# An audio tower on one core: stores issued by SyncE, wider gaps at ScalarE's waits, the tokens' first result thirty beats earlier

## The chip, the cores and the metric

The program runs on one core of one Trainium2 chip. The metric is device time in microseconds (us) of one execution. The engines are TensorE (PE, with weight loads as PEld), VectorE (DVE), ScalarE (ACT), GpSimd (POOL) and SyncE (SP). They run one instruction stream each and meet at semaphores.

## The reference

128 sequences of 256 steps and 64 channels go through a token stage, two attentions and two feed-forward layers:

```python
h = _L0_tok_ref(x, ...)                          # strided conv, norm over time and channels, PReLU -> (128, 128, 64)
h = h + _L0_attn_ref(_layernorm(h), W)           # x_ = xn triu(W)^T; (x_ xn^T) xn
h = h + _L0_ffn_ref(_layernorm(h), ...)          # product keys, below
h = h + _L1_attn_ref(_layernorm(h), ...)         # linear attention, 8 heads of 8, then a norm
h = h + _L1_ffn_ref(_layernorm(h), ...)          # 8 experts, top 2, gelu

# _L0_ffn_ref
sim = einsum('pbnhd,pkhd->pbnhk', q, pk_keys)    # 2 sides, 8 heads, 64 sub-keys
scores, idx = top_k(sim, 16)
score = scores[0][..., :, None] + scores[1][..., None, :]
final_scores, pk_idx = top_k(score, 16); final_scores = softmax(final_scores)
k = einsum('bnhk,bnhkd->bnhd', final_scores, keys_table[ind])    # 4096 rows per head
v = einsum('bnhk,bnhkd->bnhd', final_scores, values_table[ind])
out = softmax(causal(q_ k^T)) v; return out @ Wo
```

## The kernel before

**Pairs and periods.** Two sequences make a pair; there are 64 (`PAIRS`). Every engine works through periods, one per pair. In a period it interleaves the work of several pairs (`over_pairs`): `dense` and `prep` of the pair itself, `tail` and `back` of the pair before (its last beats, attention, second attention, experts, output), `select` of the next pair (sub-key products, top 16) and `front` of the one behind that (convolution to first attention).

**Beats.** The bulk of the product-key layer is done densely for six of eight heads. A period has 192 beats (`BEATS`), 32 for each such head. In beat c TensorE forms 128 x 512 sums in one of three PSUM banks (L1425, L1426, `p_s`), ScalarE takes their exponential into `ew` (L1174), VectorE masks four beats at once (L947), and nine beats later (`LAG`) TensorE multiplies the result with the value table (L1437, `p_d`). So a late exponential holds the sums three beats later, and a late mask holds the product. The mask of the beats 188 to 191, for instance, is needed for the product in beat 5 of the next period. After each head ScalarE empties `p_d` into `dense_t_sb` (L1179), and TensorE can start the next head's products only then.

**The order.** Each step of a chain yields its due beat, and `interleave` emits on each engine always the step that is due first. Nothing else sets the order: an engine runs its stream in this order, and an instruction that waits stops all behind it. The due beats of `front` are spread by shares in `FRONT`, those of `back` in `BACK` (from beat 16 to 190), those of `select` by `at_select` and `at_unit`, those of the rank matrices by `at_fill`. Steps that the text speaks of:

- `exponent` (ScalarE, due at c + 1), `mask` (VectorE, due at c + 1.5).
- `neg_kmax` (VectorE L999) and `ek_t` (ScalarE L1268, waits for it), due at `BACK["kmax"]` 101.2 and `BACK["ek"]` 104.3.
- The tokens' first result `h0` (VectorE L726 to L737, with L684 to L696): due at `FRONT["h0"]` 146.1 and 148.1. The scale that it needs comes from ScalarE's `root1` (141.2), that of its normalisation `xh1` (159.5) from `root2` (155.9).
- The rank matrices for a head: `rank_hot` (VectorE L928 twice, L935 twice), then 32 matmuls (L1388).
- The experts: 16 matmuls (L1573) and eight gelus (L1296) due at `BACK["hid"]` 171.0, 32 matmuls (L1580) at `BACK["y"]` 180.0, and on VectorE the output stage L1081, L1086 (183.0, 184.5), L1089 and L1092 (186.0), which writes `h_out` and signals `out_ready`.
- The store: ScalarE waits for `out_ready` (L1301) and issues the DMA (L1302), due at 190.0, between two exponentials.
- The queries (TensorE L1479), due at beat 1 of the period, wait for `out_ready` too, since they overwrite the bank `p_x` that the output stage reads.
- Gathered heads: GpSimd fetches rows (L642) and adds them up (L656, L659), from beats 164.5, 172, 179.5 and 187.
- SyncE loads the inputs (L535) and the value table in 48 pieces of 256 KB per period (L543) through a ring of four; piece u waits until the products of piece u - 4 are done.

## Time and profile before

| | |
|---|---|
| Median of 3 runs | 13503.45 us (13494.18 to 13523.84) |
| Profiled execution, its own time | 13459.08 us |
| Its span | 13457.3 us |
| Mean granted TensorE clock | 0.959 |
| PE / DVE / ACT / POOL busy | 89 / 82 / 75 / 49 % |
| A period in the middle | about 208 us |

The profile is of one execution. Its span is the time from the first to the last instruction; 1.8 us lie around it. A period is 192 beats, so a beat takes 1.08 us on average. L numbers are lines of the kernel before. In the timeline a number in brackets is idle time of the engine before the instruction, with what ended it. Where the text says "beat 105" it means the stretch between the sums of beat 105 and those of 106, found by counting L1426 in the timeline; in the period that is shown here beat 105 starts at 6444.9 us, beat 153 at 6495.4, beat 191 at 6541.7.

### The profile page before, as it was taken

Reading aid. Unit: us, or ns where it says so; the run is one execution under the profiler, and the core shown is the slowest. Engines: PE = TensorE matmul, PEld = TensorE weight load, DVE = VectorE, ACT = ScalarE, POOL = GpSimd, SP = SyncE. Lnnn points to the kernel's source line nnn. Section 1 sums busy time; section 2 is a strip of 40 time slices with the busy share of each in tenths; the row PEclk is TensorE's granted clock in tenths of the full one; section 3 lists DMA queues with packets and bytes.
Section 4 is the critical chain, followed back from the end, with each engine's and each line's share of the span. In section 5 each row is a group of like instructions: output and inputs, shape, how many; then the busy total and the mean of one; then the engine's idle time right before and its main releaser. Section 6 shows DMA issues by size and latency. Waiting matters only on the chain.

```text
span 13457.3 us, 332297 instructions
## 1 busy us (share of the span) xinstructions
PE 12006.3 (89%) x83744; PEld 9072.3 (67%) x83744; DVE 11075.8 (82%) x37953; ACT 10064.7 (75%) x24019; POOL 6548.1 (49%) x5160
## 2 busy tenths in 40 slices
PE   6998988989989889898998988988989899899898
PEld 4666666666666666666666666666666666666666
DVE  7888888888888888888888888888888888888885
ACT  5777777777777777777777777777777777777776
POOL 4454444544444445444454444544544445545453
PEclk9999999999999999999999999999999999999998
DMA  2222222222222222222222222222222222222222
GB/s 72 85 84 81 87 81 83 85 81 86 82 81 85 81 84 83 81 86 81 84 85 80 87 82 82 85 82 85 82 82 86 81 84 84 82 86 83 83 87 64
DMA packets 612231, 1111.70 MB, mean 83 GB/s; under 512 B 134096, under 2 KB 150992, under 8 KB 610384
## 3 DMA queue, kind: packets, MB, share of 16 engines
q1 hardware_dynamic: 461648, 816.40, 19.8%
q0 software_dynamic: 131072, 268.70, 7.1%
q8 instruction: 887, 14.53, 0.4%
q14 instruction: 928, 7.60, 0.2%
q10 hardware_dynamic: 17696, 4.46, 0.1%
HBM read 1084.90 MB, written 4.19 MB: 81 GB/s over the span
## 4 chain that ended last, share of the span: by engine, by line
PE 58%; DVE 17%; ACT 11%; DVEq 7%; issue 6%; ACTq 0%; POOL 0%; POOLq 0%
PE p_d L1437 25%; PE p_s L1425 6%; PE p_s L1426 6%; ACT ew L1174 5%; PE p_g L1388 4%; DVE ew L947 4%; PE p_f L1372 2%; PE p_x L1580 2%; PE p_x L1516 2%; PE p_x L1573 1%; DVEq L685 1%; ACT gath L1217 1%; ACT prob L1247 1%; DVE h_out L1092 1%; DVE cand L827 1%
## 5 line engine op out<-in xcount | busy, mean ns | idle before, releaser
L1174 ACT ACTIVATE ew<-p_s 128x512 f32<-128x512 f32 x12288 | 7012.6, 617 | 2393.0 <-PE p_s L1426 1882.8
L1437 PE MATMUL p_d<-ew,tab 128*128 128x256 f32 x24576 | 7739.6, 398 | 639.2 <-DVE ew L947 347.5
L642 POOL DMA_INDIRECT gath<-in_table,idx x4096 | 4947.5, 1208 | 5234.6 <-PE p_s L1426 4827.6
L947 DVE SCALAR_TENSOR_TENSOR ew<-ew 128x1024 f32<-128x1024 f32 x3072 | 4024.2, 1310 | 1483.8 <-ACT ew L1174 1389.8
L1437 PEld LDWEIGHTS p_d<-ew,tab 128*128 128x128 f32 x24576 | 3827.4, 196 | 1094.3 <-issue 908.7
L1425 PE MATMUL p_s<-mov,rank_sel 128*128 128x256 f16 x12288 | 3418.5, 278 | 439.2 <-ACT ew L1174 438.2
L1426 PE MATMUL p_s<-mov,piece_sel 128*128 128x256 f16 x12288 | 3415.4, 278 | 0.0
L656 POOL TENSOR_TENSOR gath<-gath 128x1024 f32<-128x1024 f32 (+2 forms) x768 | 1338.7, 1743 | 1538.4 <-PE p_s L1426 1443.8
L1426 PEld LDWEIGHTS p_s<-mov,piece_sel 128*128 128x128 f16 x12288 | 1221.1, 99 | 1242.8 <-issue 85.4
L1425 PEld LDWEIGHTS p_s<-mov,rank_sel 128*128 128x128 f16 x12288 | 1241.6, 101 | 1098.2 <-issue 763.9
L1217 ACT ACTIVATE gath<-gath,kv_w 128x128 f32<-128x128 f32 x4096 | 1452.2, 418 | 0.0
L928 DVE TENSOR_TENSOR rank_hot<-iota_k,rank_key 128x2048 f16<-128x2048 f16 x768 | 977.6, 1280 | 41.7 <-issue 23.4
L1388 PE MATMUL p_g<-ident_rank,rank_hot 128*128 128x128 f16 x12288 | 866.2, 227 | 117.2 <-DVE rank_hot L935 71.1
L1388 PEld LDWEIGHTS p_g<-ident_rank,rank_hot 128*128 128x128 f16 x12288 | 790.1, 102 | 178.8 <-issue 160.1
L1165 ACT CAST mov<-p_g 128x512 f16<-128x512 f32 (+1 forms) x1152 | 606.9, 527 | 170.1 <-PE p_g L1388 168.6
L935 DVE TENSOR_TENSOR rank_hot<-rank_hot,rank_val 128x1024 f16<-128x1024 f16 x768 | 523.3, 688 | 19.9 <-issue 6.4
L776 DVE FIND_INDEX8 top_i<-top,sim 128x8 uint32<-128x64 f32 x2048 | 411.5, 219 | 0.0
L768 DVE MAX8 top<-sim 128x8 f32<-128x64 f32 x2048 | 296.3, 212 | 138.2 <-ACT sim L1153 137.8
L1247 ACT ACTIVATE prob<-p_x,neg_max 128x128 f32<-128x128 f32 x1024 | 399.7, 436 | 12.1 <-DVE neg_max L972 12.1
L798 DVE FIND_INDEX8 top_i<-top,sim 128x8 uint32<-128x64 f32 x2048 | 406.9, 219 | 0.0
L784 DVE MATCH_REPLACE8 sim<-top,sim 128x64 f32<-128x64 f32 x2048 | 403.4, 207 | 0.0
L793 DVE MAX8 top<-sim 128x8 f32<-128x64 f32 x2048 | 300.9, 212 | 4.6
(234 smaller groups left out, 12275.6 us busy)
## 6 DMA issues: line engine op xcount, KB each, us to landing
tab<-in_dense_t SPq DMA_DIRECT2D x3072, 256.0 KB
gath<-in_table,idx POOLq DMA_INDIRECT x4096
xin<-in_x SPq DMA_DIRECT2D x64, 128.0 KB, 2.4
out<-h_out ACTq DMA_DIRECT2D x64, 64.0 KB, 1.7
row_consts<-in_rows SPq DMA_DIRECT2D x1, 548.0 KB, 4.2
w_sb<-in_w SPq DMA_DIRECT2D x1, 512.0 KB, 6.9
w_sb<-in_w ACTq DMA_DIRECT2D x1, 256.0 KB, 4.5
gath<-in_wqpk_t SPq DMA_DIRECT2D x1, 256.0 KB, 5.5
```

The lines of the kernel that those rows point to most:

```text
L642: G.indirect_dma_start(out=gath[:, slot, k, :], out_offset=None, in_=table[:, :], in_offset=bass.IndirectOffsetOnAxis(ap=idx[pair.par][:, ...
L656: G.tensor_tensor(gath[:, slot, 0:half, :], gath[:, slot, 0:half, :], gath[:, slot, half:2 * half, :], ALU.add).then_inc(halved, 1)
L928: V.tensor_tensor(hots[p].rearrange("t r s c i -> t (r s) c i"), iota_k[:, :].rearrange("t (c i) -> t c i", i=2)[:, None, :, :].to_broadca ...
L947: V.scalar_tensor_tensor(four[:, :, 2 * T:4 * T], four[:, :, 0:2 * T], CHOSEN, four[:, :, 2 * T:4 * T], ALU.is_gt, ALU.mult).then_inc(dens ...
L1165: A.copy(mov[mov_slot(d)][:, first:last, :].rearrange("q a t -> q (a t)"), p_g[:, 0:2 * T * (last - first)]).then_inc(bank_free, 1)
L1174: A.activation(ew[:, c % EW_RING, :], p_s[c % PS_RING][:, :], ACT.Exp).then_inc(dense_e_ready, 1)
L1217: last = A.activation(gath[:, slot, k, :], gath[:, slot, k, :], ACT.Copy, scale=kv_w[pair.par][:, HEADS * p + h, k:k + 1])
L1247: last = A.activation(prob[:, a, hp, :], px[:, a, T * hp:T * hp + T], ACT.Exp, bias=neg_max[:, h:h + 1], accum_out=row_sum[:, a, hp:hp + 1])
L1388: last = M(p_g[:, T * p:T * p + T], rank_hot[p][:, r, :, :].rearrange("t s i -> t (s i)"), ident_rank[:, r, :], start=(r == 0), stop=(r == ...
L1425: M(bank[:, 0:2 * T], rank_sel[:, c % CHUNKS, :], mov[mov_slot(d)][:, 0, :], start=True, stop=True)
L1426: M(bank[:, 2 * T:4 * T], piece_sel[:, k, :], mov[mov_slot(d)][:, MAP_OF[layout], :], start=True, stop=True).then_inc(pair_mm, 1)
L1437: last = M(p_d[:, 0:2 * T], tab[:, u % TAB_RING, i, :], ew[:, c % EW_RING, 2 * T:4 * T], start=(k == 0), stop=(k == CHUNKS - 1))
```

## The change

Stores: SyncE gets a `store` that waits for `out_ready` and issues the DMA, placed behind the 48 table pieces of the period and ahead of the next input and the next table pieces; ScalarE's wait, store and final wait go. The queries wait for a new semaphore `y_taken`, signalled by L1081, the first step of the output stage (and once ahead of the loop); the wait for `out_ready` goes to the transposes of the keys (`k_tr`, beat 16).

Due beats:

| step | before | after |
|---|---|---|
| FRONT var, root1, h0, root2 | 121.7, 141.2, 146.1, 155.9 | 105.9, 113.2, 118.0, 127.8 |
| FRONT xh1 and all behind it | 159.5 ... | the same |
| BACK ek, a, l1_x, z, h3, xn, gap, mix, hid | 104.3 ... 171.0 | each 2.0 later |
| BACK y, out | 180.0, 183.0 | 183.5, 187.0 |
| queries' copy on ScalarE | 2.0 | 2.4 |
| sub-key units 1 to 3: matmul, copy | u - 1.9, u - 0.8 | u - 4.0, u - 2.4 |
| sub-key units on VectorE | u | u + 0.4 |
| rank_hot, all four steps | | each 1.0 earlier |

```diff
-               "xin_tr:3 x2t:3 conv:8 stats:6 mean:6 dev:20 var:16 root1:4 h0:8 root2:3 xh1:4 gram:2 gram_copy:2 "
+               "xin_tr:3 x2t:3 conv:8 stats:6 mean:6 dev:7 var:6 root1:4 h0:8 root2:26 xh1:4 gram:2 gram_copy:2 "
...
-EARLY = {"queries": 1, "q_copy": 2}
-BACK = spread(TAIL_END + 1, BEATS - 2,
+EARLY = {"queries": 1, "q_copy": 2.4}
+BACK = spread(TAIL_END + 1, BEATS - 5,
...
-              "gap:5 gap_e:3 mix:6 hid:9 y:3 out:7 store")
+              "gap:5 gap_e:3 mix:6 hid:10.5 y:3.5 out")
...
+        def store(pair):
+            hold(sp, out_ready, pair.n + 1)
+            sp.dma_start(of_pair(out_pairs, pair.n), h_out[pair.par][:, :, :]).then_inc(out_done[pair.par], 16)
...
                 tables(Pair(2 * it + q + 1, it + q, 1 - q))
+                store(Pair(2 * it + q, it, q))
...
-                yield at_unit(u, 0)
+                yield at_unit(u, 0.2)
...
-                yield at_fill(d, 0) + 2 * p - 9.2
+                yield at_fill(d, 0) + 2 * p - 10.2
...
-                yield at_fill(d, 0) + p - 5.2
+                yield at_fill(d, 0) + p - 6.2
...
-                            ALU.add)
+                            ALU.add).then_inc(y_taken, 1)
...
-                yield at_unit(u, 0) - 0.8
+                yield at_unit(u, 0) - (0.8 if u == 0 else 2.4)
...
-            yield BACK["store"]
-            hold(act, out_ready, count)
-            act.dma_start(of_pair(out_pairs, pair.n), h_out[pair.par][:, :, :]).then_inc(out_done[pair.par], 16)
...
-                yield at_unit(u, 0) - 1.9
+                yield at_unit(u, 0) - (1.9 if u == 0 else 4)
...
-            if positive(done):
-                hold(pe, out_ready, done)
+            hold(pe, y_taken, done + 1)
...
             hold(pe, q_ready, count)
+            if positive(done):
+                hold(pe, out_ready, done)
```

Three places show how the streams move. In the changed kernel the same statements stand some lines further down (L1174 is L1185, L947 is L957, L1092 is L1102).

ScalarE around beat 190, before; the register and ISA rows are the waits' bookkeeping:

```order
L1173 REGISTER_ALU
L1174 ACTIVATE ew<-p_s 128x512
L1302 ISA
L1302 DMA out<-h_out 128x2x64
L1173 REGISTER_ALU
L1174 ACTIVATE ew<-p_s 128x512
```

and SyncE at the end of a period, after:

```order
L544 DMA tab<-in_dense_t 128x512
L549 ISA
L549 DMA out<-h_out 128x2x64
L536 ISA
L536 DMA xin<-in_x 128x2x128
L514 ISA
L544 DMA tab<-in_dense_t 128x512
```

The store has left ScalarE's exponentials and stands on SyncE behind the last table piece of one period and ahead of the first of the next.

VectorE at the end of the output stage (`k_t` is the experts' output buffer, L945 and L955 belong to the masks), before, where L1081 and L1086 stand six instructions further up with a mask and a normalisation of `front` between:

```order
L1089 TENSOR_REDUCE xh<-k_t 128x128
L1091 ISA
L1092 TENSOR_TENSOR h_out<-h,xh 128x128 [waits out_done0]
L945 REGISTER_ALU
L947 SCALAR_TENSOR_TENSOR ew<-ew 128x4x256 [waits dense_e_ready]
L926 REGISTER_ALU
L928 TENSOR_TENSOR rank_hot<-iota_k,rank_key 128x2048 [waits map_tr]
```

after:

```order
L1091 TENSOR_TENSOR k_t<-p_x,row_consts 128x1024 [waits y_mm]
L1096 TENSOR_TENSOR k_t<-k_t,w_full 128x1024
L955 REGISTER_ALU
L957 SCALAR_TENSOR_TENSOR ew<-ew 128x4x256 [waits dense_e_ready]
L1099 TENSOR_REDUCE xh<-k_t 128x128
L1101 ISA
L1102 TENSOR_TENSOR h_out<-h,xh 128x128 [waits out_done0]
L936 REGISTER_ALU
L938 TENSOR_TENSOR rank_hot<-iota_k,rank_key 128x2048 [waits map_tr]
L955 REGISTER_ALU
L957 SCALAR_TENSOR_TENSOR ew<-ew 128x4x256 [waits dense_e_ready]
```

The mask that stood behind the output's last step (that of the beats 184 to 187) now stands ahead of its third; one mask (180 to 183) and the normalisation of `front` have moved ahead of its first.

VectorE at beats 117 to 120 (`prob_t` is `l1_x`, `f_tmp`, `yn` and the last `h` are the tokens' first result), before:

```order
L855 TENSOR_TENSOR kv_w<-fin_d,fin_r 128x256
L1011 TENSOR_TENSOR prob_t<-p_x,head_of 128x1024 [waits l1_o_mm]
L862 CAST pos_h<-pos_i 128x64
L866 TENSOR_TENSOR sim<-iota_c,pos_h 128x1664
L945 REGISTER_ALU
```

after:

```order
L865 TENSOR_TENSOR kv_w<-fin_d,fin_r 128x256
L736 ISA
L694 SCALAR_TENSOR_TENSOR f_tmp<-p_f,f_rstd 128x2 [waits f_root_ready]
L696 SCALAR_TENSOR_TENSOR f_tmp<-f_tmp,f_rstd 128x2
L698 SCALAR_TENSOR_TENSOR f_rstd<-f_tmp,f_rstd 128x2
L739 SCALAR_TENSOR_TENSOR yn<-yn,f_rstd,row_consts 128x64 x2
L1021 TENSOR_TENSOR prob_t<-p_x,head_of 128x1024 [waits l1_o_mm]
L743 SCALAR_TENSOR_TENSOR neg_part<-yn,row_consts 128x128
L745 SCALAR_TENSOR_TENSOR h<-yn,neg_part 128x128
L703 BN_STATS f_stats<-h 128x6 x2
L706 BN_AGGR f_mv<-f_stats 128x2 x2
L872 CAST pos_h<-pos_i 128x64
```

The eleven instructions of `h0` stand here now, thirty beats ahead of where they stood.

## Rows read from the trace of the kernel before

**Rows 1.** Totals: the page's first part (busy us, share of the span, instructions).
```profile
PE 12006.3 (89%) x83744; PEld 9072.3 (67%) x83744; DVE 11075.8 (82%) x37953; ACT 10064.7 (75%) x24019; POOL 6548.1 (49%) x5160
```
**Rows 2.** Waits, whole run: who waited for whom; us, times, longest us.
```profile
PE p_s L1425 <- ACT ew L1174: 438.2, 315, 5.2
PE p_d L1437 <- DVE ew L947: 347.5, 258, 4.2
ACT ew L1174 <- DVE h_out L1092: 345.2, 61, 5.9
ACT ek_t L1268 <- DVE neg_kmax L999: 269.6, 63, 4.4
DVE top L768 <- ACT sim L1153: 137.8, 126, 3.8
```
**Rows 3.** Windows of one period, its beats 84 to 154.
```profile
core 0: us, PE busy (x) PEld busy (x) DVE busy (x) ACT busy (x) POOL busy (x), PEclk, DMA share, GB/s
6429.00:6453.00 24.00, 18.90 (x128) 14.56 (x127) 22.25 (x106) 15.51 (x37) 12.37 (x10) 0.94 0.31 92
6453.00:6470.00 17.00, 17.00 (x136) 13.43 (x134) 11.54 (x29) 14.51 (x38) 7.46 (x7) 0.99 0.31 91
6470.00:6500.00 30.00, 24.20 (x166) 17.69 (x165) 27.08 (x82) 21.80 (x53) 9.10 (x7) 0.96 0.28 87
```
**Rows 4.** Timeline, beats 103 to 106: start, duration, instruction, count, [idle before, releaser].
```profile
6443.50 0.27 PE L1425 MATMUL p_s<-mov,rank_sel 128*128 128x256 f16 x1
6444.15 0.27 PE L1425 MATMUL p_s<-mov,rank_sel 128*128 128x256 f16 x1
...
6450.22 1.19 PE L1437 MATMUL p_d<-ew,tab 128*128 128x256 f32 x2 [2.84 <-ACT dense_t_sb L1179]
...
6448.87 0.37 ACT L1268 ACTIVATE ek_t<-p_x,neg_kmax 128x128 f32<-128x128 f32 x1 [4.35 <-DVE neg_kmax L999]
```
**Rows 5.** Timeline, TensorE at beat 153.
```profile
6498.46 1.19 PE L1437 MATMUL p_d<-ew,tab 128*128 128x256 f32 x2 [2.84 <-DVE ew L947]
```
**Rows 6.** Timeline, TensorE at the end of the period (beats 191, 0, 1).
```profile
6547.05 0.37 PE L1425 MATMUL p_s<-mov,rank_sel 128*128 128x256 f16 x1 [4.65 <-ACT ew L1174]
...
6548.41 2.08 PE L1479 MATMUL p_x<-xh_t,wq_sb 64*128 64x128 f32 x16
```
**Rows 7.** Windows behind the three long waits: granted clock (PEclk) and busy time.
```profile
6450.30:6453.80 3.50, 3.50 (x22) 2.97 (x23) 2.43 (x17) 1.27 (x4) 0.94 (x1) 0.56 0.00 0
6498.50:6505.00 6.50, 6.50 (x22) 4.46 (x23) 5.58 (x28) 2.87 (x8) 0.00 (x0) 0.53 0.00 0
6545.50:6551.00 5.50, 3.95 (x23) 2.95 (x24) 5.34 (x5) 2.53 (x5) 4.92 (x4) 0.50 0.20 60
```
**Rows 8.** Timeline, VectorE and GpSimd in the output stage, beats 180 to 0.
```profile
6534.35 1.22 DVE L1081 TENSOR_TENSOR k_t<-p_x,row_consts 128x1024 f32<-128x1024 f32 x1 [2.64 <-PE p_x L1580]
6535.65 1.79 DVE L1086 TENSOR_TENSOR k_t<-k_t,w_full 128x1024 f32<-128x1024 f32 x1
...
6540.43 1.90 DVE L1089 TENSOR_REDUCE xh<-k_t 128x128 f32<-128x1024 f32 x1
...
6542.41 3.14 DVE L1092 TENSOR_TENSOR h_out<-h,xh 128x128 f32<-128x128 f32 x1
...
6543.03 2.36 POOL L656 TENSOR_TENSOR gath<-gath 128x1024 f32<-128x1024 f32 x1
...
6547.84 1.74 DVE L928 TENSOR_TENSOR rank_hot<-iota_k,rank_key 128x2048 f16<-128x2048 f16 x1
6549.50 1.47 DVE L947 SCALAR_TENSOR_TENSOR ew<-ew 128x1024 f32<-128x1024 f32 x1
```
**Rows 9.** Groups by shape: an addition shaped like L1092, elsewhere; mean ns.
```profile
L1027 DVE TENSOR_TENSOR h<-h,xh 128x128 f32<-128x128 f32 x64 | 18.7, 293 | 4.8
```
**Rows 10.** DMA issues: KB each, median us from issue to landing.
```profile
xin<-in_x SPq DMA_DIRECT2D x64, 128.0 KB, 2.4
wq_sb<-in_wq SPq DMA_DIRECT2D x1, 256.0 KB, 5.0
```

More of the change, by code:

```diff
@@ L502, in build @@
     y_mm = sem("y_mm")
+    y_taken = sem("y_taken")
     out_ready = sem("out_ready")
@@ L556, in _ @@
             tables(Pair(n, n // 2, n % 2))
+            store(Pair(n - 1, (n - 1) // 2, (n - 1) % 2))
+        store(Pair(PAIRS - 1, (PAIRS - 1) // 2, 1))
+        for p in range(2):
+            sp.wait_ge(out_done[p], 16 * (PAIRS // 2) + 16)
     @block.gpsimd
@@ L1096, in _ @@
         dve.wait_ge(pool_consts, POOL_CONSTS)
+        dve.sem_inc(y_taken, 1)
         V.reciprocal(rank_inv[:, :], rank_left[:, :])
@@ L1146, in select @@
             count = pair.n + 1
-            yield EARLY["q_copy"] + 1
+            yield EARLY["q_copy"] + 0.8
             act.wait_ge(xh2_tr, count)
@@ L1299, in back @@
             A.preload_act_table_set("natural_log_exp_and_others")
-            yield BACK["store"]
-            hold(act, out_ready, count)
-            act.dma_start(of_pair(out_pairs, pair.n), h_out[pair.par][:, :, :]).then_inc(out_done[pair.par], 16)
         over_pairs(act, front, select, prep, tail, back, weigh, sums, dense)
-        for p in range(2):
-            act.wait_ge(out_done[p], 16 * (PAIRS // 2) + 16)
     @block.tensor
```

2 rows, old and new, of the table BACK are left out of this document.

## The prediction

> **What bounds the kernel.** I began with the totals: TensorE is busy 12006 us of 13457, VectorE 11076 [rows 1]. No engine is full, so the time above TensorE's own work is waiting, and a static order makes it repeat in each of the 64 periods. Next the waits of the whole run, to see what holds TensorE [rows 2]: 438 us for exponentials (L1425), 348 us for masks (L1437). The same list shows ScalarE idle for 345 us at its store's wait (61 times, 5.7 us each) and for 270 us at `ek_t` (63 times, 4.3 us each). Then the timeline of one period, to see where TensorE loses how much. A beat in the steady stream takes 0.65 us, from one L1425 to the next [rows 4], though the period's mean is 1.08. Three places stand out: 2.84 us in beat 105, with ScalarE idle 4.35 us for `neg_kmax` ahead of the exponentials and of the emptying of `p_d` [rows 4]; 2.84 us in beat 153 for a late mask [rows 5]; 4.65 us at the end of the period, for exponentials that stand behind the store [rows 6]. Behind each of the three the granted clock is 0.50 to 0.56, the lower of its two levels (1.2 instead of 2.4 GHz) [rows 7], while in a stretch without a long wait it is 0.99 [rows 3]. At the lower level the work takes twice as long, so half of TensorE's busy time there is lost: 3.50 x 0.44 = 1.5 us, 6.50 x 0.47 = 3.1 us and 3.95 x 0.50 = 2.0 us [rows 7]. Waits and clock together make 2.8 + 1.5, 2.8 + 3.1 and 4.65 + 2.0, some 17 us of a period of 208.
>
> The Trainium skill ("TensorE: Matmul & The Clock Gate", What's actually happening) has the clock gated down by default and released by activity; the trace agrees: the three low stretches begin in TensorE's three longest waits.
>
> **The store, and the end of the period.** ScalarE's wait and issue go; its exponentials of beats 189 to 191 follow their sums at once. Gain on TensorE: the 4.65 us [rows 6] and the 2.0 us of clock. What is late next is VectorE. `out` is due four beats later, and the mask of beats 188 to 191 stands behind all of it. From the end of the experts' last matmuls VectorE has 1.22 + 1.79, a mask of 1.47, 1.90, 3.14, `rank_hot` 1.74 and that mask 1.47 [rows 8]: 12.7 us. TensorE reaches the product that needs it after 13.5 beats of 0.65 (8.8), the queries (2.08 at half clock [rows 6], so 1.0), and about two beats' worth (1.3, an estimate) for a transposition and the first sub-key matmuls: 11.1 us. So a new wait of 1.6 us in beat 5. The term is 4.65 + 2.0 - 1.6 = 5.0 us, times 61 = **305 us**. Bounds: 2.0 (the clock stays low and the new wait is 2.7) and 6.6 (no new wait).
>
> **The store on SyncE.** It costs nothing as long as the table is early. The last step of the output ends 1.22 + 1.79 + 1.47 + 1.90 + 3.14 = 9.5 us after those matmuls [rows 8]. Queued behind the store are the input of a later pair and the next period's first table pieces, for which only TensorE waits. Landing takes between 2.4 us (128 KB) and 5.0 us (256 KB, at the start, with many others) [rows 10]; with about 1 us for issuing store, input and piece, the first piece lands 13 to 15.5 us after the matmuls. Its product is due four beats and a rank matrix after the product above, at 12.7 + 2.6 + 1 = 16 us. Cover: 0.8 to 3.4 us. The wait of `k_tr` for `out_ready` in beat 16 lies later still: nothing.
>
> **Beats 84 to 154: `ek` two beats later, `h0` thirty earlier, `rank_hot` one earlier.** ScalarE now does two exponentials and empties `p_d` before it waits for `neg_kmax`, which VectorE reaches no sooner. The products of beat 105 then wait only for their mask: about 0.8 us is left of the 2.84, and the 1.5 us of clock comes back: 3.5 us by beat 109. At beat 153 the wait (2.84) and the clock (3.1) could go too, 9.5 us in all, if VectorE let them. It doesn't. In rows 3 it is busy 22.3 of 24, 11.5 of 17 and 27.1 of 30 us: full before 6453 and after 6470, idle for 5.5 us only between, while TensorE is busy all of those 17 us. The moved block, eleven small instructions and their drains, some 2.8 us by its share of the third stretch (an estimate), goes from the full stretch to the idle one. So the mask in beat 153 comes at least 2.8 us earlier (the block alone) and at most 5.5 us (all idle time filled, which TensorE's 3.5 us of head start makes possible). I take 4.4, four fifths of the idle time, since a mask still waits for its exponential now and then. Behind beat 154 VectorE stays full up to beat 160, so the clock's 3.1 us there is not a second gain. New short waits of about 1.5 us appear near beats 125 and 133, where the block delays masks; they are in the 4.4. Times 63 = **277 us**. Bounds: 2.0 (only the wait in beat 105) and 7.
>
> **The rest.** The sub-key units' matmul and copy come earlier: VectorE's 138 us of waiting for `sim` [rows 2] goes, 2.2 us per period, but TensorE does not wait there, so 0.3 us (0 to 2). The experts two beats later move eight gelus and two table loads behind a copy that frees a bank: -0.2 us (-1.5 to 0.5). Together 63 x 0.1 = **6 us**.
>
> **Sum.** 305 + 277 + 6 = 588 us. Against the profiled execution that is 13459 - 588 = 12871; the median of the runs lies 44 us above that execution, which gives 13503 - 588 = **12915 us**.
>
> **Rivals.**
> - *VectorE is not the limit* (0.14). If its instructions pack tighter than I count, TensorE gains 6.6 x 61 + 7 x 63 = 844 us: 12660. For it: VectorE is idle 18% of the run [rows 1]. Against: the full stretches in rows 3.
> - *The clock stays low* (0.13). The shorter waits that remain could still pull it down: the first term loses 2.0, the second about 1: 588 - 122 - 63 = 403, so 13100. For it: a remaining wait of 1.6 us stands in beat 5. Against: rows 3 have 0.99 over 17 us with small waits around.
> - *The port shared with GpSimd* (0.10). L1092 takes 3.14 us [rows 8], an addition of its shape elsewhere 0.29 [rows 9]; it ends when GpSimd's first sum (L656) does. Later by four beats, the output stage can meet the second sum as well. Then its last step takes up to 2.4 us more and TensorE waits that long in beat 5: 588 - 2.4 x 61 = 442, so 13061. The Trainium skill ("SBUF — State Buffer", Who interferes with whom) calls the shared ports an exclusive lock, held for a whole instruction; by that rule the step waits out any sum that began before it.
> - *Only the store pays* (0.07). The masks eat what `ek` and `h0` give: 305 - 100 = 200 us, 13300.
> - *The queue of SyncE makes it slower* (0.03). Table pieces stand behind a wait for VectorE. If the last output step comes more than 3.4 us later than I count, TensorE waits for the first piece, us for us; it decides from there, and more than 3.4 + 9.6 = 13 us late it takes all the gain. At 15 us late: 61 x 2 = 120 us slower, 13625. Against it: no row of VectorE in the output stage waits that long [rows 8].
> - *Nothing happens* (0.03). The order of another engine holds the exponentials as before: 13500.
>
> **The numbers.** My forecast has 0.50. The chance of faster by over 0.2% (27 us, about what a measurement of this kernel can tell from no change) is 0.50 + 0.14 + 0.13 + 0.10 + 0.07 = 0.94; within it 0.03; slower 0.03. The range goes from 12700, close to the first rival and to both upper bounds, to 13200, past the clock and the port; it leaves out the last three cases and little of the first.
>
> **What the profile will show.** No ScalarE wait for L1092; TensorE's wait for exponentials down from 438 us to under 150; `ek_t`'s wait at or above 4 us still, but without TensorE behind it; TensorE's wait for masks not much smaller than 348, and moved to beats 5, 125 and 133; VectorE's share up to about 86%; granted clock above 0.98; periods of 198 to 200 us. I am wrong if a piece of `tab` ends TensorE's waits, if the clock still falls three times a period, or if the period stays above 205 us.

## The result and the profile after

| | before | after |
|---|---|---|
| Median | 13512.54 us of 4 runs (13494.18 to 13523.84) | 13668.67 us of 4 runs (13642.79 to 13680.1) |
| Ratio | | 1.0114, 95% interval 1.0095 to 1.0134 |
| Profiled span | 13457.3 us | 13640.9 us |
| Mean granted clock | 0.959 | 0.953 |
| A period | 208.2 us | 211.0 us |

The change makes the kernel 1.1% slower. The forecast was 12915 us, 4.4% faster, with a range up to 13200: wrong in sign. L1185 is L1174 of before, L957 is L947, L1102 is L1092, L1009 is L999, L1443 is L1437, L712 is L702, L925 is L915, L666 is L656, L1356 is L1350, L1431 and L1432 are L1425 and L1426.

First the waits of the whole run after the change, the view of [rows 2] (us in total, times, longest):

```profile
ACT ew L1185 <- PE p_s L1432: 2492.4, 2328, 5.5
...
PE p_d L1443 <- DVE ew L957: 581.9, 332, 5.3
PE p_s L1431 <- ACT ew L1185: 200.4, 304, 3.1
ACT ek_t L1279 <- DVE neg_kmax L1009: 181.0, 63, 2.9
PE p_f L1356 <- DVE xh L712: 161.9, 61, 24.6
PE p_g L1394 <- ACT kv L1196: 156.1, 62, 2.6
```

ScalarE's wait for the output stage is gone, and TensorE's wait for exponentials has fallen from 438 to 200 us. In their place TensorE waits 582 us for masks (348 before), and two small lines have grown: the gram matmul L1356 waits for the normalisation `xh1` 61 times (4 times before), and the matmuls of the rank matrices wait 156 us for `kv` (40 before). So time was moved, and more than was gained. Where, a table by beats tells; it is made from the starts of each beat's second sum (L1426 before, L1432 after) in the timeline, averaged over periods 4 to 59:

| beats | before | after | difference |
|---|---|---|---|
| 0 to 15 | 16.6 | 20.0 | +3.4 |
| 15 to 84 | 73.0 | 72.9 | -0.1 |
| 84 to 109 | 26.8 | 24.7 | -2.1 |
| 109 to 124 | 13.6 | 12.1 | -1.5 |
| 124 to 152 | 25.5 | 29.4 | +3.9 |
| 152 to 163 | 13.8 | 8.3 | -5.5 |
| 163 to 170 | 6.2 | 13.6 | +7.5 |
| 170 to 184 | 22.5 | 23.9 | +1.4 |
| 184 to 192 | 10.2 | 6.1 | -4.2 |
| period | 208.2 | 211.0 | +2.8 |

The places of the forecast did gain: beats 152 to 163 give 5.5 us, beats 184 to 192 give 4.2 (and the first four beats of the next period 1.8 more), beats 84 to 109 give 2.1 of the 3.5 forecast there. The largest loss, beats 163 to 170, is in no term of it. There the timeline of one period after shows VectorE and GpSimd:

```profile
6613.75 2.67 DVE L712 TENSOR_SCALAR xh<-h,f_mv,f_rstd 128x64 f32<-128x64 f32 x2
6616.35 0.55 DVE L921 TENSOR_TENSOR rank_val<-rank_n,rank_inv 128x384 f16<-128x384 f16 x1
6616.81 2.38 DVE L925 CAST rank_key<-top_i 128x192 f16<-128x192 uint32 x4
6619.35 1.28 DVE L957 SCALAR_TENSOR_TENSOR ew<-ew 128x1024 f32<-128x1024 f32 x1
...
6614.03 2.34 POOL L666 TENSOR_TENSOR gath<-gath 128x1024 f32<-128x1024 f32 x1 [17.00 <-PE p_s L1432]
6616.55 1.46 POOL L666 TENSOR_TENSOR gath<-gath 128x512 f32<-128x512 f32 x1 [0.18 <-POOL gath L666]
6618.19 0.72 POOL L666 TENSOR_TENSOR gath<-gath 128x256 f32<-128x256 f32 x1 [0.18 <-POOL gath L666]
```

and TensorE in the same stretch:

```profile
6616.57 0.30 PE L1356 MATMUL p_f<-ident,xh 128*128 128x128 f32 x1 [2.24 <-DVE xh L712]
...
6620.93 1.19 PE L1443 MATMUL p_d<-ew,tab 128*128 128x256 f32 x2 [3.18 <-DVE ew L957]
```

GpSimd's first sum starts when TensorE reaches beat 164 (it waits for L1432). VectorE has just begun the two small L712. They take 2.67 us together and end 0.05 us behind the sum's first instruction (6614.03 + 2.34); the four casts L925 take 2.38 us. TensorE waits 2.24 us for `xh`, then 3.18 us for the mask behind the casts. The groups by shape give the mean of one (columns: busy us, mean ns, then idle time), before:

```profile
L915 DVE CAST rank_key<-top_i 128x192 f16<-128x192 uint32 x256 | 54.0, 275 | 0.0
L702 DVE TENSOR_SCALAR xh<-h,f_mv,f_rstd 128x64 f32<-128x64 f32 x128 | 38.5, 344 | 5.1
```

and after:

```profile
L712 DVE TENSOR_SCALAR xh<-h,f_mv,f_rstd 128x64 f32<-128x64 f32 x128 | 158.5, 1281 | 5.0
L925 DVE CAST rank_key<-top_i 128x192 f16<-128x192 uint32 x256 | 148.5, 639 | 0.0
L1102 DVE TENSOR_TENSOR h_out<-h,xh 128x128 f32<-128x128 f32 x64 | 88.0, 1375 | 7.7 <-issue 5.2
```

The two cost 214 us more over the run, with the same shapes and counts, while L1102 has come down to 1375 ns from the 3.14 us of [rows 8]. Windows after, at the two worst places and in one stretch without a long wait (columns as in [rows 3]):

```profile
6453.00:6460.00 7.00, 6.96 (x34) 5.11 (x35) 6.85 (x22) 2.76 (x5) 5.63 (x6) 0.57 0.37 113
6620.90:6627.50 6.60, 6.58 (x24) 4.65 (x25) 6.15 (x13) 3.24 (x8) 0.00 (x0) 0.59 0.05 8
...
6595.00:6613.00 18.00, 17.67 (x114) 12.87 (x113) 16.54 (x64) 16.68 (x38) 1.19 (x1) 1.00 0.28 80
```

The clock is at its lower level behind beats 5 and 165, as it was behind beats 191 and 153 before [rows 7], and full in the 18 us from beat 139 on. By these rows beats 164 and 165 cost 2.24 + 3.18 us of waiting and 6.58 x 0.41 = 2.7 us of clock.

### The profile page after: what moved, and what is told of

It is laid out like the page before. It is cut to its first block, busy times and chain, and to the rows that moved or that the text cites. A ratio compares the mean times of both kernels' runs of the same rounds, so it can differ in the third digit from the quotient of the medians.

```text
span 13640.9 us, 332361 instructions
## 1 busy us (share of the span) xinstructions
PE 12101.2 (89%) x83744; PEld 9104.8 (67%) x83744; DVE 11000.6 (81%) x37953; ACT 10110.7 (74%) x24019; POOL 6393.2 (47%) x5160
## 4 chain that ended last, share of the span: by engine, by line
PE 47%; DVE 23%; DVEq 11%; ACT 10%; issue 8%; ACTq 0%; POOL 0%; another core or an unknown queue 0%; POOLq 0%
PE p_d L1443 21%; DVE ew L957 6%; PE p_s L1432 5%; PE p_s L1431 5%; ACT ew L1185 5%; PE p_g L1394 5%; DVEq L942 3%; DVE rank_hot L938 2%; PE p_x L1523 2%; DVEq L695 2%; PE p_f L1378 1%; DVEq L885 1%; ACT gath L1228 1%; PE p_x L1580 1%; PE p_x L1509 1%
## 5 line engine op out<-in xcount | busy, mean ns | idle before, releaser
L1185 ACT ACTIVATE ew<-p_s 128x512 f32<-128x512 f32 x12288 | 7060.9, 610 | 2722.8 <-PE p_s L1432 2492.4
L1443 PE MATMUL p_d<-ew,tab 128*128 128x256 f32 x24576 | 7825.6, 401 | 612.0 <-DVE ew L957 581.9
L957 DVE SCALAR_TENSOR_TENSOR ew<-ew 128x1024 f32<-128x1024 f32 x3072 | 3867.3, 1261 | 1996.3 <-ACT ew L1185 1722.4
L1443 PEld LDWEIGHTS p_d<-ew,tab 128*128 128x128 f32 x24576 | 3857.0, 198 | 1121.6 <-issue 945.4
L1431 PE MATMUL p_s<-mov,rank_sel 128*128 128x256 f16 x12288 | 3438.1, 280 | 209.4 <-ACT ew L1185 200.4
L1432 PE MATMUL p_s<-mov,piece_sel 128*128 128x256 f16 x12288 | 3433.4, 279 | 0.4 <-issue 0.4
L1432 PEld LDWEIGHTS p_s<-mov,piece_sel 128*128 128x128 f16 x12288 | 1231.2, 100 | 1303.9 <-issue 158.8
L1431 PEld LDWEIGHTS p_s<-mov,rank_sel 128*128 128x128 f16 x12288 | 1255.7, 102 | 840.8 <-issue 499.9
L666 POOL TENSOR_TENSOR gath<-gath 128x1024 f32<-128x1024 f32 (+2 forms) x768 | 1228.5, 1600 | 1188.4 <-PE p_s L1432 1093.3
L1394 PE MATMUL p_g<-ident_rank,rank_hot 128*128 128x128 f16 x12288 | 897.1, 231 | 229.4 <-ACT kv L1196 156.1
L1394 PEld LDWEIGHTS p_g<-ident_rank,rank_hot 128*128 128x128 f16 x12288 | 821.2, 105 | 294.2 <-issue 271.3
L945 DVE TENSOR_TENSOR rank_hot<-rank_hot,rank_val 128x1024 f16<-128x1024 f16 x768 | 510.2, 692 | 19.9 <-issue 6.4
L1258 ACT ACTIVATE prob<-p_x,neg_max 128x128 f32<-128x128 f32 x1024 | 384.5, 405 | 12.1 <-DVE neg_max L982 12.1
L1196 ACT ACTIVATE kv<-p_g,fin_r 128x128 f32<-128x128 f32 x768 | 241.6, 374 | 86.6 <-PE p_g L1452 86.6
L1378 PE MATMUL p_f<-score_w,xh_t 64*128 64x512 f32 x512 | 283.6, 634 | 24.7 <-ACT xh_t L1160 22.3
```

What stands on the lines that cost most here:

```text
L666: G.tensor_tensor(gath[:, slot, 0:half, :], gath[:, slot, 0:half, :], gath[:, slot, half:2 * half, :], ALU.add).then_inc(halved, 1)
L945: V.tensor_tensor(hots[p][:, :, 0, :, :], hots[p][:, :, 0, :, :], rank_val[:, DENSE * p + d, :, None, :].to_broadcast([T, TOPK, SUBKEYS // ...
L957: V.scalar_tensor_tensor(four[:, :, 2 * T:4 * T], four[:, :, 0:2 * T], CHOSEN, four[:, :, 2 * T:4 * T], ALU.is_gt, ALU.mult).then_inc(dens ...
L1185: A.activation(ew[:, c % EW_RING, :], p_s[c % PS_RING][:, :], ACT.Exp).then_inc(dense_e_ready, 1)
L1394: last = M(p_g[:, T * p:T * p + T], rank_hot[p][:, r, :, :].rearrange("t s i -> t (s i)"), ident_rank[:, r, :], start=(r == 0), stop=(r == ...
L1431: M(bank[:, 0:2 * T], rank_sel[:, c % CHUNKS, :], mov[mov_slot(d)][:, 0, :], start=True, stop=True)
```

## The experiments

**Theory P**: TensorE, without its wait in beat 153, reaches beat 164 before VectorE has done `xh1`; GpSimd's first sum then starts in the middle of it, and shares something with it that only one of them can have. **Theory H**: the output stage four beats later is paid in beats 0 to 15. **Rival**: VectorE is the bound, and each gain is given back at the next mask, whatever GpSimd does.

**1. The parts.** `s1_store`: before, with the store on SyncE alone. (Its expectation speaks of `y_taken`; the kernel that ran still had the queries behind `out_ready`. The whole part came later, in s12.)

```diff
+                store(Pair(2 * it + q, it, q))
...
-            yield BACK["store"]
-            hold(act, out_ready, count)
-            act.dma_start(of_pair(out_pairs, pair.n), h_out[pair.par][:, :, :]).then_inc(out_done[pair.par], 16)
```

> Before, with the stores on SyncE and the queries behind y_taken, and no due beat changed. Theory P (the loss of the change comes from GpSimd's sum at beat 164, which takes the port shared with VectorE while xh1 is being normalised) and theory H (it comes from the experts and the output stage being due later): this part alone is good, the 4.65 us wait at beat 191 and its 2.0 us of low clock go, part comes back in beat 5: 4 to 5 us per period, so about 13230 us. Theory S (the store's move itself costs, through VectorE's late masks or SyncE's queue): 13500 or more, with a new wait in beats 4 to 12 as long as the old one.

Measured: 13480.73 us, ratio 0.9989 (0.998 to 0.9999). Beats 184 to 192 gain 3.3 us; 0 to 15 lose 1.3, 15 to 84 1.1, 84 to 109 0.9. A wait at the period's end was removed, and the same time comes up again in pieces.

`s2_front`: before, with FRONT of after alone.

```diff
-               "... dev:20 var:16 root1:4 h0:8 root2:3 xh1:4 ..."
+               "... dev:7 var:6 root1:4 h0:8 root2:26 xh1:4 ..."
```

> Before, with the FRONT shares of the change and nothing else (h0 thirty beats earlier). Theory P: the wait in beat 153 and its clock (5.8 us per period) go, and a wait of 5 to 8 us appears in beats 164 and 165, with L702 taking 2 to 3 us beside GpSimd's L656: 13450 to 13650 us. Theory V (VectorE's order is better by h0's move, GpSimd has no part in it): 13200 to 13300 us, no new wait at 164. Theory H: the same as V.

Measured: 13837.56 us, ratio 1.0248 (1.023 to 1.0265). Beats 152 to 163 gain 5.7 us, 163 to 170 lose 7.1, 124 to 152 lose 2.0, 170 to 184 lose 1.6. The waits of this kernel (line numbers of before) show the long wait at the gram too:

```profile
PE p_d L1437 <- DVE ew L947: 428.6, 316, 5.3
...
PE p_f L1350 <- DVE xh L702: 137.3, 50, 24.6
```

So the move of `h0` is the part that makes the kernel slower, and it brings the wait at the gram. `s3_no_front`: after, with FRONT of before (the same diff turned round).

> The change with the FRONT shares of before (h0 back at beats 146 and 148). Theory P: TensorE is held in beat 153 again (5.8 us), so GpSimd's sum starts after xh1 is ready and the waits of beats 164 and 165 go (7.9 us): 2 us per period faster than the change, about 13540 us, with L712 back at 0.3 us each. Theory V: undoing a good part makes it slower, 13900 us or more.

Measured: 13384.81 us, ratio 0.991 (0.9887 to 0.9933), 155 us below the expected time. The rest of the change is worth 0.9%. The forecast had 311 us for it in its first and last terms, and 3.5 us per period (220 us) by beat 109 in the second: 3.9%. Beats 163 to 170 take 8.4 us here (6.2 before), so not all of their loss has gone. L712 is short again in all but 6 of its 128 instructions, but the sum now meets `rank_hot` and a mask. In one period:

```profile
6471.47 1.22 DVE L957 SCALAR_TENSOR_TENSOR ew<-ew 128x1024 f32<-128x1024 f32 x1
6472.61 3.38 DVE L938 TENSOR_TENSOR rank_hot<-iota_k,rank_key 128x2048 f16<-128x2048 f16 x1
...
6471.65 3.26 POOL L666 TENSOR_TENSOR gath<-gath 128x1024 f32<-128x1024 f32 x1 [21.63 <-PE p_s L1432]
...
6478.82 0.67 PE L1443 MATMUL p_d<-ew,tab 128*128 128x256 f32 x2 [2.77 <-DVE ew L957]
```

**2. GpSimd's sum.** `s4_sums_later`: after, first sum 3.5 beats later, the others 2.5, 1.5 and 0.5.

```diff
-    return SUMS_AT + 7.5 * m
+    return SUMS_AT + 3.5 + 6.5 * m
```

> The change, with GpSimd's four sums due at beats 168, 174.5, 181 and 187.5 in place of 164.5, 172, 179.5 and 187. Nothing moves on the other four engines. Theory P: xh1 is ready before the first sum starts, so the waits in beats 164 and 165 and the low clock behind them go: 5 to 7 us per period, about 13300 us, L712 at 0.3 us each. Theories V and H: no change within 0.3%, 13669 us, and L712 late for another reason.

Measured: 13267.88 us, ratio 0.9828 (0.9812 to 0.9845): a number in the due beats of GpSimd, an engine with half its time idle, takes 400 us from the changed kernel. VectorE and TensorE at beat 164 in this run:

```profile
6417.78 0.54 DVE L712 TENSOR_SCALAR xh<-h,f_mv,f_rstd 128x64 f32<-128x64 f32 x2
...
6418.70 0.76 DVE L925 CAST rank_key<-top_i 128x192 f16<-128x192 uint32 x4
6419.61 1.22 DVE L957 SCALAR_TENSOR_TENSOR ew<-ew 128x1024 f32<-128x1024 f32 x1
...
6418.47 0.30 PE L1356 MATMUL p_f<-ident,xh 128*128 128x128 f32 x1
...
6421.13 0.67 PE L1443 MATMUL p_d<-ew,tab 128*128 128x256 f32 x2 [1.48 <-DVE ew L957]
```

The same instructions take 0.54 and 0.76 instead of 2.67 and 2.38 us; beats 163 to 170 go from 13.6 to 7.6 us. `s5_xh1_earlier` takes the other side away: the sum stays, `xh1` comes earlier.

```diff
-               "... root2:26 xh1:4 ..."
+               "... root2:20 xh1:10 ..."
```

> The changed kernel with the tokens' normalisation xh1 due six beats earlier (153.5 instead of 159.5), everything else as changed, GpSimd's sums where they were. Theory P (the first sum, due at beat 164.5, and VectorE's L712 and L925 share a port, and TensorE waits for them in beat 164): xh1 is done before the sum begins, so L712 is back at about 0.3 us each, the wait of 2.2 us for xh and most of what follows it goes; rank_key's casts still meet the sum. Beats 163 to 170 take 8 to 9 us instead of 13.6; period about 206, time 13350 (13270 to 13450). Rival (what costs is that gram comes before the sum or that the product there waits for its mask, whatever the port does): beats 163 to 170 stay at 13 us, time 13600 to 13700.

Measured: 13464.48 us, ratio 0.9977 (0.9968 to 0.9987), 110 us above the expected middle; beats 163 to 170 take 9.8 us, where 8 to 9 were expected. L712 is back at 311 ns. But now the sum meets the mask of beats 156 to 159:

```profile
6507.09 3.15 DVE L957 SCALAR_TENSOR_TENSOR ew<-ew 128x1024 f32<-128x1024 f32 x1
6510.16 2.28 DVE L938 TENSOR_TENSOR rank_hot<-iota_k,rank_key 128x2048 f16<-128x2048 f16 x1
...
6506.67 2.48 POOL L666 TENSOR_TENSOR gath<-gath 128x1024 f32<-128x1024 f32 x1 [18.04 <-PE p_s L1432]
6509.33 2.03 POOL L666 TENSOR_TENSOR gath<-gath 128x512 f32<-128x512 f32 x1 [0.18 <-POOL gath L666]
```

A mask of 1.22 us takes 3.15, and TensorE waits 2.58 us for it. The cost is not in `xh1` alone; it is in whatever VectorE does when the sum starts, if TensorE is close behind. `s7_sums_only` is the control: the kernel before, with the sums of s4.

> The kernel before with only GpSimd's sums moved (first sum 3.5 beats later, second 2.5, third 1.5, fourth 0.5), as the control for the run that moved them in the changed kernel. Theory P: before, TensorE came to beat 164 after VectorE had finished xh1, so there is no collision to take away: 13450 to 13530, the same as before within 0.3%. Rival (the sums stand in a bad place whatever the change does): as much gain as in the changed kernel, 2.9%, 13100.

Measured: 13524.26 us, ratio 1.0024 (1.0014 to 1.0034). Where TensorE comes late to beat 164, next to nothing is to be had there (beats 163 to 170 go from 6.2 to 5.9 us), and the run is 0.2% slower. Theory P stands: from both sides, and with its control. What the two engines share these runs do not show by themselves; they show that an instruction of one is held while one of the other runs.

**3. What is left.** `s9_nofront_sums`: s4 with FRONT of before.

> The changed kernel with the sums later and the tokens' result h0 back at beat 146. With the sums out of the way h0's move should be worth what it gains in beats 152 to 158 (5 us) less what it costs in beats 124 to 152 (about 3 us): undoing it loses 2 us per period, 13268 + 63 x 2 = 13390 (13330 to 13450). Rival (h0's move is worth nothing even without the collision, since VectorE has the same work): 13270 or less.

Measured: 13277.95 us, ratio 0.9838 (0.9821 to 0.9854), the same as s4. So the move of `h0` is worth nothing even without the collision: 4.5 us gained in beats 152 to 163 against 3.0 lost in 124 to 152 and 1.5 in 163 to 170. In this the rival was right and I was not.

`s8_out_back`: s4 with the experts, their second layer and the output stage due as before.

```diff
-              "gap:5 gap_e:3 mix:6 hid:10.5 y:3.5 out")
+              "gap:5 gap_e:3 mix:4 hid:9 y:3 out:7 end")
```

> The changed kernel with the sums later, and the experts, their second layer and the output stage due as before (170.9, 180.0, 183.0 instead of 173.0, 183.5, 187.0); ek to mix stay two beats later. Theory H (the output stage four beats later makes the masks of beats 184 to 191 late, TensorE waits in beats 5 and 12 and the clock falls): beats 4 to 15 go from 16.3 back to about 12.3 us, beats 170 to 184 lose 1 us; against that up to 1 us in the last beats. Period 200 to 201, time 13000 (12930 to 13120). Rival (beats 4 to 15 are long because TensorE arrives there sooner, with VectorE behind, wherever the output stage is due): 13268 as without this edit, within 50 us.

Measured: 13273.68 us, ratio 0.984 (0.9823 to 0.9856), no gain. Beats 0 to 15 fell from 20.6 to 17.4 us as theory H says, but 184 to 192 rose by 2.2 and 15 to 84 by 1.7. VectorE and GpSimd, beats 180 to 187 of this run:

```profile
6430.98 2.70 DVE L1096 TENSOR_TENSOR k_t<-k_t,w_full 128x1024 f32<-128x1024 f32 x1
6433.83 2.07 DVE L957 SCALAR_TENSOR_TENSOR ew<-ew 128x1024 f32<-128x1024 f32 x1
...
6430.21 2.38 POOL L666 TENSOR_TENSOR gath<-gath 128x1024 f32<-128x1024 f32 x1
6432.77 2.04 POOL L666 TENSOR_TENSOR gath<-gath 128x512 f32<-128x512 f32 x1 [0.18 <-POOL gath L666]
```

Here the third sum, 1.5 beats later, meets the output stage: L1096 takes 2.67 us on average over this run, 1.23 in s4. `s10_sums_two` puts the second, third and fourth sum back:

```diff
-    return SUMS_AT + 3.5 + 6.5 * m
+    return SUMS_AT + (3.5, 7.5, 15, 22.5)[m]
```

> As the run with the sums later and the output stage back, but only the first sum is later (168); the others stand where they stood (172, 179.5, 187). There the third sum (181) began with the output stage: L1096 took 2.70 us instead of 1.79, the mask behind it 2.07 instead of 1.23, and TensorE lost 2 us in beat 189 and 1.5 us in beats 17 to 20. Theory P: with the third sum ahead of the output stage both come back: beats 189 to 192 at 3 us, beats 15 to 84 at 72.9; period 201.5, time 13050 (12980 to 13150). Rival (the output stage meets a sum wherever it stands, and the masks of beats 180 to 191 stay late): 13274 as before within 50 us, with L1102 longer again in place of L1096.

Measured: 13018.33 us, ratio 0.9675 (0.9661 to 0.9689), within 32 us of the expected middle. Beats 184 to 192 gain 1.2 us and 15 to 84 2.6, and L1096 is down to 1.60 us. The three sums were not moved one by one.

`s11_h0_early` moves `h0` into a hole of VectorE.

```diff
-               "... dev:7 var:6 root1:4 h0:8 root2:26 ..."
+               "... dev:5 var:5 root1:4 h0:8 root2:29 ..."
```

> As s10, with the tokens' result h0 due at 114.4 instead of 118.0, so that it comes into the 1.8 us in which VectorE is idle ahead of the mask of beats 112 to 115, instead of between that mask and the next. Theory V (each block of VectorE costs what it delays the next mask by; h0 at 118 adds 2.9 us ahead of the mask that beat 125 needs, more than TensorE's lead): the wait in beat 125 goes from 1.85 to under 0.5, beats 124 to 152 from 29.4 to 27 us; 60 x 2.4 = 140 us less than s10. Rival (VectorE has as much to do on both sides of that mask, the wait moves to beat 117 or stays): within 30 us of s10.

Measured: 12920.22 us, ratio 0.9603 (0.9588 to 0.9618). VectorE and TensorE around beat 124, in s10:

```profile
6253.90 1.23 DVE L957 SCALAR_TENSOR_TENSOR ew<-ew 128x1024 f32<-128x1024 f32 x1 [1.80 <-ACT ew L1185]
...
6256.32 0.16 DVE L694 SCALAR_TENSOR_TENSOR f_tmp<-p_f,f_rstd 128x2 f32<-128x2 f32 x1
...
6261.76 2.36 DVE L957 SCALAR_TENSOR_TENSOR ew<-ew 128x1024 f32<-128x1024 f32 x2
...
6263.28 0.67 PE L1443 MATMUL p_d<-ew,tab 128*128 128x256 f32 x2 [1.85 <-DVE ew L957]
```

and VectorE in s11:

```profile
6190.54 0.15 DVE L694 SCALAR_TENSOR_TENSOR f_tmp<-p_f,f_rstd 128x2 f32<-128x2 f32 x1
...
6194.29 1.23 DVE L957 SCALAR_TENSOR_TENSOR ew<-ew 128x1024 f32<-128x1024 f32 x1 [0.16 <-issue]
...
6199.16 2.36 DVE L957 SCALAR_TENSOR_TENSOR ew<-ew 128x1024 f32<-128x1024 f32 x2
```

The hole of 1.80 us ahead of the mask is filled, and between the two masks 4.87 us pass instead of 7.86 (from start to start). TensorE does not wait in beat 125 any more; beats 124 to 152 take 27.4 instead of 29.4 us. The same block, 3.6 beats sooner, is worth another 0.7%.

`s12_store_full`: before, with the whole store part (store on SyncE, queries behind `y_taken`, `k_tr` behind `out_ready`).

> The kernel before with the whole of the store's part of the change and nothing else: the store on SyncE, the queries behind y_taken, k_tr behind out_ready (s1_store had the store alone, with the queries still behind out_ready). The prediction's term for this part with the output stage four beats later was 5.0 us per period. Theory G (what TensorE gains at the period's end is given back in beats 4 to 15, since VectorE's masks are not earlier): 13400 to 13480, with beats 4 to 15 one to two us longer than before and the wait for the exponentials in beat 191 gone. Rival (with the output stage left at beat 183 the masks keep up, and the whole 6.6 us is gained): 13500 - 400 = 13100.

Measured: 13373.42 us, ratio 0.9942 (0.9928 to 0.9956). By the ratio 78 us less than before: close to theory G, 27 us below its range, and far from its rival. Beats 184 to 192 gain 3.4 us and 0 to 4 another 0.5; beats 4 to 15 give 1.6 back. In half of the periods the output stage meets the fourth sum (30 of 64 L1102 take over 1.5 us), and the mask behind it pays:

```profile
6492.96 3.13 DVE L1102 TENSOR_TENSOR h_out<-h,xh 128x128 f32<-128x128 f32 x1
6496.25 2.20 DVE L957 SCALAR_TENSOR_TENSOR ew<-ew 128x1024 f32<-128x1024 f32 x1 [0.17 <-issue]
...
6492.61 0.94 POOL L652 DMA_INDIRECT gath<-in_table,idx  x1 [0.30 <-issue]
6493.56 2.37 POOL L666 TENSOR_TENSOR gath<-gath 128x1024 f32<-128x1024 f32 x1
6496.11 1.26 POOL L666 TENSOR_TENSOR gath<-gath 128x512 f32<-128x512 f32 x1 [0.18 <-POOL gath L666]
...
6498.75 0.67 PE L1443 MATMUL p_d<-ew,tab 128*128 128x256 f32 x2 [3.76 <-DVE ew L957]
```

TensorE, free of the store, waits 3.76 us in beat 1 of this period instead of 4.65 in beat 191 [rows 6]. That is the worst case, in 14 of the 56 periods; the others wait up to 1.5 us in beat 5 or not at all there.

`s13_no_gaps`: s11 with the sub-key units and `rank_hot` due as before.

```diff
-                yield at_unit(u, 0) - (1.9 if u == 0 else 4)
+                yield at_unit(u, 0) - 1.9
...
-                yield at_fill(d, 0) + 2 * p - 10.2
+                yield at_fill(d, 0) + 2 * p - 9.2
```

> As s11_h0_early, with the wider gaps undone: the sub-key units' matmul, copy and first step on VectorE, and all four steps of rank_hot, due as in the kernel before. The prediction put the gaps at 0.1 us per period net, so 12930. Segments say more: beats 15 to 84 are 1.0 us shorter than before in s10 and s11, and there only the units and rank_hot differ from the kernel with the whole store part alone. Theory U (the gaps are worth that 1 us, since TensorE then does not stand behind the copy of a unit): 12920 + 63 = 12985 (12950 to 13030). Rival (the gaps only trade one stall for another): 12920 within 25 us. If rank_hot one beat earlier costs masks: faster than 12900.

Measured: 13051.83 us, ratio 0.9665 (0.9653 to 0.9677); s11 had 0.9603. The kernel before took 13446.89 us beside s10, s11 and s12, and 13506.52 us here, so the ratios are to be compared: the gaps are worth 0.9665 - 0.9603 = 0.6%, 84 us, somewhat more than the 65 expected. Beats 15 to 84 take 74.0 us without them and 72.0 with them (72.9 in s12, run beside s11, which has no such gaps).

The share of each stage in all of it, us per period, worked out as above (s10 and s11 were run beside a kernel before that took 0.4% less, up to 0.9 us of a period):

| beats | before | after | s2 | s4 | s8 | s10 | s11 |
|---|---|---|---|---|---|---|---|
| 0 to 15 | 16.6 | 20.0 | 17.2 | 20.6 | 17.4 | 17.4 | 17.6 |
| 15 to 84 | 73.0 | 72.9 | 73.0 | 72.8 | 74.5 | 71.9 | 72.0 |
| 84 to 124 | 40.4 | 36.8 | 40.8 | 36.5 | 36.6 | 36.6 | 36.1 |
| 124 to 152 | 25.5 | 29.4 | 27.5 | 29.4 | 29.4 | 29.4 | 27.4 |
| 152 to 163 | 13.8 | 8.3 | 8.1 | 8.3 | 8.3 | 8.3 | 8.3 |
| 163 to 170 | 6.2 | 13.6 | 13.2 | 7.6 | 7.6 | 7.6 | 7.6 |
| 170 to 192 | 32.7 | 30.0 | 34.4 | 29.5 | 31.1 | 29.8 | 30.0 |
| period | 208.2 | 211.0 | 214.4 | 204.8 | 204.9 | 200.9 | 198.9 |

s11 beats both kernels: 4.0% faster than before, 5.1% than the change (0.9603 / 1.0114 = 0.949). Its mean granted clock is 0.988.

## Why the prediction was wrong

**The step that failed: "Behind beat 154 VectorE stays full up to beat 160, so the clock's 3.1 us there is not a second gain."** This is where the working of the term for beats 84 to 154 stopped, and beats 160 to 170 were put at nothing, without a reason. A gain on TensorE is also a shift against VectorE, and GpSimd's sum is released by a beat of TensorE. In the next ten beats the sum met `xh1` and the casts, which the change had left in place, and these beats took 7.5 us more. s4 takes 6.0 of the 7.5 back by moving the sum, s5 3.8 by moving `xh1` (and loses 1.1 in beats 152 to 163); s2 has 7.1 with the move of `h0` alone, s3 2.3 without it. No term and no rival looked at beats 160 to 170, though the masks and L1356 were there to be followed.

The term's own size came out near, partly by luck: 4.4 us forecast by beat 154, 2.9 measured there, and 2.1 + 1.5 - 3.9 + 5.5 = 5.2 us by beat 163. The difference is the very clock that the sentence excludes: beats 154 to 160 gain 2.3 us. Against that, beat 105 gave less than its 3.5 us. TensorE waits 1.17 us there for the mask, not 0.8, and behind it the clock still falls in 38 of 56 periods (periods 4 to 59, here and below; counted where the granted clock of the 2.5 us behind the beat is under 0.8).

**The end of the period, 5.0 us forecast.** It gave 4.2 - 3.4 = 0.8 us. The gain itself came: from beat 184 to beat 4 of the next period 6.0 us of the 6.65 forecast. What was mis-sized is the loss behind it, 1.6 us forecast and 5.2 measured in beats 4 to 15. The wait of 1.6 us in beat 5 was right: it is 1.75 in the period shown, by TensorE's timeline, and 1.3 on average.

```profile
6453.03 1.19 PE L1443 MATMUL p_d<-ew,tab 128*128 128x256 f32 x2 [1.75 <-DVE ew L957]
```

The term had nothing for the clock behind this wait, and "the 2.0 us of clock" are lost again there: 0.57 over 7.0 us by the window above, 6.96 x 0.43 = 3.0 us in such a period. The clock falls so in 39 of 56 periods and costs 1.9 us on average. In beat 12 TensorE waits once more, 1.2 us on average (L1452, for ScalarE's copy `mov`). This was the rival *the clock stays low*, at 0.13; for this term it was the likelier case. The output stage four beats later was counted only as the wait in beat 5. It cost more: s8, with the experts and the output stage due as before, has beats 0 to 15 3.2 us shorter than s4; the two were not moved apart from each other. The store part with the output stage where it was (s12) is worth 0.0058 x 13500 = 78 us, against the 305 of the term.

**The port.** The mechanism of the rival *the port shared with GpSimd* is the one that decided, at about its price (2.4 us forecast for one collision, 2.24 measured on L1356), in another place and more than once. It looked only at L1092, since that was the long row before, and at "later by four beats". The Trainium skill ("SBUF — State Buffer", Who interferes with whom) names `cast` and `tensor_scalar` among the instructions of VectorE that can contend with GpSimd, and says that one with two SBUF inputs does so when the GpSimd instruction reads SBUF. The trace agrees: L712 is a tensor_scalar (344 to 1281 ns), L925 a cast (275 to 639 ns), and the mask, which reads two halves of `ew`, takes 3.15 us instead of 1.22 in s5. Read as a list to look for around each of the four sums, not as a remark on L1092, it would have shown the place. In L1102 itself the change gave something back: 2626 ns on average before, 1375 after.

**The rest, 0.1 us forecast.** The wider gaps are worth 84 / 64 = 1.3 us per period (s13), above the 0.3 forecast and within its 0 to 2; they show in beats 0 to 84. Beats 170 to 184 lose 1.4 us, where I had 0.2 for the experts two beats later. Not all of it is theirs: s8, with the experts back, is 0.7 us shorter there than s4, and s2, which leaves them in place, loses 1.6.

**SyncE.** Right: no piece of `tab` ends a wait, and the store costs nothing there.

**What the profile was to show.** Right: no ScalarE wait for the output, masks that take over, waits near beats 5 and 125. Wrong: exponentials under 150 us (200), masks near 348 us (582), `ek_t` at 4 us (2.9), VectorE's share up to 86% (81), clock above 0.98 (0.953), periods of 198 to 200 us (211). The text named a period above 205 us, and a clock that still falls three times a period, as what would make it wrong: both came, the clock falling behind beats 5, 105, 125 and 165, not in every period behind the first three. That s11 ends at 12920 us is no support for 12915: it needs three edits more.

Left open: which wait of beats 0 to 84 the gaps take away; how s8 comes to lose 1.7 us in beats 15 to 84 (s7 does too; both have the third sum on top of the output stage, with L1086 or L1096 at 2.7 us, while s4 and s9, with the later sums but a later output stage, lose nothing there); and how much of the 3.9 us in beats 124 to 152 is the stage `z` two beats later (s3, with `h0` back, has 0.8 there, s2 2.0), which was not tried alone.

## What to carry to other kernels

In a static order a gain on the engine ahead is a shift of everything that it releases: after costing an edit, follow the shifted engine through the whole next period, and at each step that it releases on a third engine ask what the second is doing then. Every long GpSimd instruction belongs on that list, with the casts, tensor_scalars and two-input operations of VectorE within its length; its due beat is as good a knob as that of the step you move. A wait that is replaced by a shorter one may give no clock back, and a place for a block of small instructions is a hole in the waiting of its engine just ahead of a mask, not a stretch in which it is on average idle.

## What the runs showed of the hardware

- A VectorE instruction of 0.3 us becomes some 2.4 us (the pair's 2.67 less the first's 0.3) when a GpSimd addition starts beside it, and ends within 0.1 us of that addition's end (6616.42 and 6616.37 in the period shown after). The addition itself was no longer (2.34 us, against a mean of 2388 ns before and after).
- The order of starting decides between a mask and the addition. In s5 the mask starts 0.42 us behind the addition and takes 3.15 us instead of 1.22. In s3 the mask starts 0.18 us ahead of it, keeps its 1.22 us, and the addition takes 3.26 (above; 24 such cases in that run, the addition at 3.11 to 3.42 us). With L712 a start just ahead is not enough: in all runs together it was held 79 times when it began 0.04 to 0.06 us ahead of the sum's first addition, as in the period shown (6613.98 and 6614.03), and kept its 0.31 us 51 times when it began 0.13 to 0.22 us ahead.
- It is not always the one that starts first that has its way. In s12 L1102 starts at 6492.96, 0.60 us ahead of the addition (6493.56), and still ends 0.16 us after it (6496.09 and 6495.93). A gather's DMA issue on GpSimd (6492.61 to 6493.55) lies under its start, and may have held it. In all runs here L1102 (L1092 before) ran into such an addition from ahead 230 times, each time with a gather's issue under its start, so they can't tell.
- The clock fell to its lower level behind a wait as short as 1.75 us (the period shown after), where the waits before were 2.84 and 4.65. It does not do so each time: the changed kernel's wait of 1.9 us in beat 125 has it behind it in 28 of 56 periods, the wait of 1.5 us in beat 165 of s4 in none.
